# Output projection of the first attention: plain fp32 matmuls in place of split halves

## What is computed

```python
q = einsum('bqm,muh->bquh', h, Wq) + bq     # h = layernorm(x), 32 heads of 64
k = einsum('bkm,mvh->bkvh', h, Wk) + bk     # 8 heads of 64
v = einsum('bkm,mvh->bkvh', h, Wv) + bv
q, k = rope(q) * SCALE, rope(k) * SCALE
scores = where(|i - j| <= 128, q k^T, NEG)  # a sink logit per head is appended
probs = softmax([scores, sink])[..., :-1]
out = einsum('buqk,bkuh->bquh', probs, v)
x = x + einsum('bquh,uhm->bqm', out, Wo) + bo
```

## Time and profile before

| | |
|---|---|
| runs | 1245.62, 1250.10, 1249.98 us (median 1249.98) |
| the profiled execution | 1249.12 us |
| its span, first to last instruction | 1247.3 us |
| mean granted TensorE clock | 0.939 of full speed |
| attention_0 | from 0 to about 378 us of the span |
| steps in its steady part | one each 9.8 to 10.2 us, four in 39.54 us |

### The profile page before, as it was taken

The page is one execution under the profiler, slowest core; times in us unless marked ns, Lnnn a source line. Parts: engine busy times, 40 slices in busy tenths (PEclk is TensorE's granted clock), DMA queues, the critical chain, the costliest instruction groups (busy, mean ns, idle before and its releaser), DMA issues. The chain is left out here.

```text
span 1247.3 us, 21375 instructions
## 1 busy us (share of the span) xinstructions
PE 1052.3 (84%) x7014; PEld 833.8 (67%) x7016; DVE 802.0 (64%) x2260; ACT 646.6 (52%) x1583; POOL 448.6 (36%) x408
## 2 busy tenths in 40 slices
PE   4789999999988986699993799999999977786767
PEld 3556666666665655588882588788887855575556
DVE  5656666666644565355557867677676745489983
ACT  2166676766663751243331566767676642234532
POOL 5456565655634331000002433433343300106730
PEclk8999999999998996799996899999999998898878
DMA  4250212101005000444430001010110000000001
GB/s 135 66 162 18 52 44 51 44 19 35 2 2 193 1 2 0 91 117 111 105 71 13 9 14 34 21 34 17 30 34 21 17 1 0 1 26 26 26 28 45
DMA packets 27246, 53.54 MB, mean 43 GB/s; under 512 B 4565, under 2 KB 11797, under 8 KB 26788
## 3 DMA queue, kind: packets, MB, share of 16 engines
q1 hardware_dynamic: 27172, 52.60, 15.5%
HBM read 42.56 MB, written 1.63 MB: 35 GB/s over the span
## 5 line engine op out<-in xcount | busy, mean ns | idle before, releaser
L382 POOL TENSOR_TENSOR sb_a_P<-sb_a_P,sb_a_rec 128x512 f32<-128x512 f32 x128 | 130.5, 1040 | 134.7 <-DVE sb_a_rec L572 134.7
L459 ACT ACTIVATE sb_a_P<-sb_a_nS,sb_a_nm 128x257 f32<-128x257 f32 x256 | 129.0, 509 | 24.4 <-DVE sb_a_nm L561 24.3
L561 DVE CUSTOM_DVE_ANT_0 sb_a_nS<-a_pS,sb_a_mask,sb_a_nsink 128x256 f32<-128x256 f32 x256 | 107.7, 479 | 15.5 <-PE a_pS L685 15.5
L1723 ACT ACTIVATE sb_a_t<-a_pp,sb_a_w 64x512 f32<-64x512 f32 x128 | 87.5, 684 | 49.4 <-PE a_pp L142 48.1
L468 ACT COPY sb_xn<-a_pT 128x512 f32<-128x512 f32 x128 | 73.7, 576 | 74.7 <-PE a_pT L699 74.5
L142 PE MATMUL a_pp<-sb_x_high,sb_a_w_low 128*128 128x512 f32 x188 | 87.1, 464 | 29.2 <-POOL sb_a_w_low L1661 20.3
L699 PE MATMUL a_pT<-sb_ident,sb_a_P 128*128 128x128 f32 x512 | 82.0, 283 | 18.4 <-ACT sb_xn L468 10.5
L1793 DVE SCALAR_TENSOR_TENSOR sb_a_t<-a_pp,sb_a_w,sb_a_cs 128x512 f32<-128x512 f32 x64 | 47.8, 746 | 73.9 <-ACT sb_a_t L1723 73.9
L699 PEld LDWEIGHTS a_pT<-sb_ident,sb_a_P 128*128 128x128 f32 x512 | 54.4, 142 | 52.1 <-issue 42.0
L142 PE MATMUL a_pY<-sb_a_wo_high,sb_a_OT_low 128*128 128x256 f32 x256 | 79.2, 309 | 7.6 <-DVE sb_a_OT_low L135 5.3
L130 ACT CAST sb_a_OT_high<-a_pO 128x256 fp32r<-128x256 f32 (+1 forms) x96 | 42.6, 444 | 78.1 <-PE a_pO L1936 39.2
(11 more groups left out here) (359 smaller groups left out, 3242.8 us busy)
## 6 DMA issues: line engine op xcount, KB each, us to landing
sb_m_cw<-m_table SPq DMA_DIRECT2D x17, 512.0 KB
sb_a_kr<-sb_a_kall SPq DMA_DIRECT2D x56, 128.0 KB, 2.4
sb_f_w<-f_w SPq DMA_DIRECT2D x12, 384.0 KB, 3.0
sb_m_gu<-m_gu SPq DMA_DIRECT2D x17, 256.0 KB, 6.5
sb_a_w<-a_w SPq DMA_DIRECT2D x16, 257.0 KB, 2.7
sb_m_dn<-m_dn SPq DMA_DIRECT2D x17, 128.0 KB, 6.7
sb_a_w<-a_w SPq DMA_DIRECT2D x8, 259.0 KB, 2.7
sb_a_wo<-a_wo SPq DMA_DIRECT2D x8, 256.0 KB, 2.6
```

The source lines that it names most:

```text
L382: nc.gpsimd.tensor_tensor(part, part, rec[b % 2][:, h, :].rearrange("p (q o) -> p q o", o=1) .to_broadcast([P, 2, S]), ALU.mult).then_inc( ...
L459: out = nc.scalar.activation(Pm[b % 2][:, h, qt, 0:S + 1], nS[:, h, qt, 0:S + 1], ACT.Exp, bias=nm[b % 2][:, h, qt:qt + 1], scale=-1.0, ac ...
L561: out = nc.vector.tensor_tensor_reduce(nS[:, h, qt, 0:S], pS[h][:, qt * S:(qt + 1) * S], wmask[:, qt, :], -1.0, nsink[par][:, h:h + 1], AL ...
L1723: out = nc.scalar.activation(t2[n][a, :, :].rearrange("p b s -> p (b s)"), pp[n][b, :], ACT.Identity, bias=bias[b])
```

## The change

The output projection no longer works on split halves. OT is one fp32 tile for each parity, which ACT copies out of pO; the DVE and POOL subtractions and the ACT rounding of wo are gone; project_out reads wo as it was loaded and issues two plain fp32 matmuls for each half where it issued six fp32r ones. Since wo is now read by the matmuls themselves, the load of wo[g] into its buffer waits for projected instead of wo_split.

```diff
-        both = parts("wo", [P, 2 * KD * D])
-        wos = [[g[:, i * KD * D:(i + 1) * KD * D] for g in both] for i in range(2)]
-        wks = both
+        wks = parts("wk", [P, 2 * KD * D])
...
-        OT = [parts(f"OT{i}", [P, NC]) for i in range(2)]
+        OT = [sb(f"OT{i}", [P, NC]) for i in range(2)]
...
                 sp.dma_start(w[g % 2][:, :], src["a0_w"][g]).then_inc(w_in[g % 2], 16)
-                sp.wait_ge(wo_split, g - 1)
+                sp.wait_ge(projected, (g - 1) * NB)
                 sp.dma_start(wo[g % 2][:, :], src["a0_wo"][g]).then_inc(wo_in[g % 2], 16)
...
-                    if b == 1:
-                        wo_low(G, par)
...
-            def high_OT(G, b):
+            def evac_OT(G, b):
                 act.wait_ge(weighed, G * (2 * NB) + (2 * b + 2))
                 if some(G, b, 2):
                     act.wait_ge(projected, G * NB + (b - 1))
-                high_of(nc, OT[b % 2][0][:, :], pO[:, :]).then_inc(OT_high, 1)
+                nc.scalar.copy(OT[b % 2][:, :], pO[:, :]).then_inc(OT_ready, 1)
...
                     if some(G, b, 2):
-                        high_OT(*lagged(G, b, 2))
-                    if b == 1:
-                        wo_to_high(G, par)
+                        evac_OT(*lagged(G, b, 2))
...
-            def low_OT(G, b):
-                dve.wait_ge(OT_high, G * NB + (b + 1))
-                low_of(nc, OT[b % 2][1][:, :], pO[:, :], OT[b % 2][0][:, :]).then_inc(OT_ready, 1)
...
-            low_OT(A0_G - 1, NB - 2)
             add_y(A0_G - 1, NB - 3)
-            low_OT(A0_G - 1, NB - 1)
             add_y(A0_G - 1, NB - 2)
...
                     if b == 0:
-                        pe.wait_ge(wo_split, G + 1)
+                        pe.wait_ge(wo_in[par], halves(G))
...
                 for p in range(2):
-                    out = split_product(nc, pY[:, qt * D:(qt + 1) * D],
-                                        [g[:, p * S + qt * P:p * S + (qt + 1) * P] for g in OT[b % 2]],
-                                        [g[:, p * D:(p + 1) * D] for g in wos[par]], start=(p == 0), stop=(p == 1))
+                    out = nc.tensor.matmul(pY[:, qt * D:(qt + 1) * D], OT[b % 2][:, p * S + qt * P:p * S + (qt + 1) * P],
+                                           wo[par][:, p * D:(p + 1) * D], start=(p == 0), stop=(p == 1))
```

More of the change, by code:

```diff
@@ L266, in attention_0 @@
                                                    sem("normed"))
-        turnedP, PT_ready, weighed, OT_high, OT_ready = (sem("turnedP"), sem("PT_ready"), sem("weighed"), sem("OT_high"),
-                                                         sem("OT_ready"))
+        turnedP, PT_ready, weighed, OT_ready = sem("turnedP"), sem("PT_ready"), sem("weighed"), sem("OT_ready")
         projected, added, bo_in, rstd_ready = sem("projected"), sem("added"), sem("bo_in"), sem("rstd_ready")
-        w_high, w_split, wo_high, wo_split = sem("w_high"), sem("w_split"), sem("wo_high"), sem("wo_split")
+        w_high, w_split = sem("w_high"), sem("w_split")
         wk_high, wk_split, wv_high, wv_split = sem("wk_high"), sem("wk_split"), sem("wv_high"), sem("wv_split")
@@ L357, in w_low @@
                 low(w_high, G + 1, w[par][:, 0:A0_NQ], [g[:, :] for g in ws[par]], w_split)
-            def wo_low(G, par):
-                low(wo_high, G + 1, wo[par][:, :], wos[par], wo_split)
             def rotate(n, tt, out, done):
@@ L431, in w_to_high @@
                 high_of(nc, ws[par][0][:, :], w[par][:, 0:A0_NQ]).then_inc(w_high, 1)
[L433 to L439, removed]
             act.wait_ge(wk_in, 32)
@@ L491, in _ @@
                 body(G, G % 2, last=(G == A0_G - 1))
-            high_OT(A0_G - 1, NB - 2)
+            evac_OT(A0_G - 1, NB - 2)
             for h in range(A0_R):
                 evac_PT(A0_G - 1, NB - 1, h)
-            high_OT(A0_G - 1, NB - 1)
+            evac_OT(A0_G - 1, NB - 1)
         @block.vector
@@ L588, in body @@
                 for b in range(NB):
-                    if some(G, b, 2):
-                        low_OT(*lagged(G, b, 2))
                     for h in range(A0_R):
```

## The result

The changed kernel takes 1271.16 us (median of 4, 1268.55 to 1273.39) against 1250.04 us for the kernel before (median of 4): a ratio of 1.0177, 95% interval 1.0144 to 1.0209, 21.1 us slower. The profiled execution took 1272.70 us with a span of 1270.9, which is 23.6 us over the one of before.

A forecast was written before the change was run, and what follows sets the result against it. ACT's chain was taken to bound the head of each attention_0 step, PE the tail. 10.0 + 4.6 + 1.5 - 1.1 = +15.0 us on 1249.12 gave 1264 us, range 1257 to 1274.

The forecast's parts named there:

- the end of the stage: Last output projection of attention_0: with the vector work gone, the last add starts earlier, -1.1 us.
- The products: project_out in attention_0: a half of two plain fp32 matmuls takes 0.86 us, hidden under ACT's chain, worth 0.
- Rival (c): Stall plus dearer product bare in project_out, 4 or 17 us: 1268 to 1281; chance 0.08 for over 1274.
- (b): Head of a step paced by PE; plain matmuls save 9 us, plus 1.1 at the end: 1239 without stall; chance 0.07.
- The removed vector work: Subtractions on DVE and POOL and casts on ACT in attention_0 lie in slack, worth 0 in the steps.
- The moved wait, g = 2: SP's later wait before loading wo[2] delays w[3], so ACT's evac_PT in step (1, 3) comes late: +10.0 us.
- The moved wait, g = 3 to 6: SP's later wait delays w[g + 1] in four later groups, +1.15 us each, +4.6 in all, bounds 4 to 8.
- The clock: PE's idling in step (1, 3) drops its clock to 1.2 GHz, +1.5 us, bounds 0 and 3.

The follow-up runs named there:

- extra-matmul run: Changed kernel with SP loading wo last, plus one plain fp32 matmul more in every half of project_out: 1263.34 us, ratio 1.0139.
- fetch-ahead run: Changed kernel with the 13 fetches for later stages issued ahead of SP's wait for projected: 1259.48 us, ratio 1.0093.
- w-before-keys run: Changed kernel with the load of w[g + 1] issued ahead of the eight key copies, behind wo[g] and the fetches: 1255.62 us, ratio 1.0068.
- wait-alone run: Kernel before, products still split, with only SP's wait before loading wo[g] changed from wo_split to projected: 1276.36 us, ratio 1.0211.

## Why the prediction was right, and by how much it fell short

The time, 1271, lies in the range of 1257 to 1274, and the mechanism was the one forecast. The size was not: 21.1 us measured between medians, 23.6 between the profiled executions, where the sum said 15.0. That 1271 still lies in the range is in part luck: the later groups went 1.4 us over their bounds of 4 to 8 us even without the clock, the end of the stage gave back less than the 1 us counted on, and the total kept inside because g = 2 stayed 2 us below its own upper bound.

**The products, worth 0: right.** The half costs 0.86 us, as the run with one more matmul shows where nothing hides it. Passing from transposes to plain matmuls costs the 0.08 us that was the upper bound: 202.14 - 201.65 = 0.49 us against 0.41 in the earlier trace rows. Sum 1.35 under a chain of 1.42. Of the 0.15 us to spare there 0.07 are left, and the extra-matmul run confirms it with 0.06. Rival (c) fell with it, and so did (b): nothing in a quiet step moved by more than 0.02 us. The three passes of the split product, beside (c), are this kernel's own code: split_product with its three fp32r matmuls of 0.12 us.

**The removed vector work, worth 0 in the steps: right.** The end of the stage was put at -1.1. The part reckoned, from the last copy of pO to the last add, is 1.08 us shorter:

```profile
397.89 0.59 ACT L458 COPY sb_a_OT<-a_pO 128x512 f32<-128x512 f32 x1 [2.51 <-PE a_pO L683]
398.53 1.99 PE L695 MATMUL a_pY<-sb_a_wo,sb_a_OT 128*128 128x256 f32 x8 [0.69 <-ACT sb_a_OT L458]
400.56 0.69 DVE L562 TENSOR_TENSOR sb_x<-a_pY,sb_x 128x512 f32<-128x512 f32 x1 [3.00 <-PE a_pY L695]
```

That is 2.67 us, against 3.75 in the earlier trace rows. But the copy itself starts 15.26 us behind the last step's first transposes, where it was 14.82: in the drain, where ACT has no exponentials left, a plain half delays what follows it. Net -0.6; half of the term of -1.1 was lost there.

**The moved wait, g = 2.** Up to the issue the working held: SP noticed projected 2.95 us behind the step's transposes (2.94 said), the fetches took 7.7 us (8.0), the keys 5.25 (5.97), w[3] left 16.4 us behind them (17.3). The term that was mis-sized is the landing: 2.65 us taken from w on an idle queue, 5.9 measured, since the fetches were still being moved (DMA share 0.53 from 127.80 to 141.50, rows below; 3.0 us with the fetches long done). The row that showed it, m_dn's 5.3 us in the earlier trace rows, stood in the bounds and not in the sum. evac_PT came 12.4 us late, not 10.0. The fetch-ahead run takes the fetches away, the w-before-keys run the keys, and each shows its part.

**The moved wait, g = 3 to 6.** 1.15 us each were said, 4.6 in all; the steps grew by 10.6. In step (2, 3) evac_PT came 181.19 - 167.72 = 13.47 us behind the transposes of (2, 2), where 10.47 is due and 11.6 was said. The key copies took 6.54, 6.26, 5.59 and 4.95 us to issue against 5.1, w landed after 2.9, 2.8, 2.8 and 3.5 against 2.65, and w's own issue comes 0.1 us behind the keys. The bounds, 4 to 8 us for the four, didn't reach it. The step that fell short is the same for both: durations of issues and landings were taken from a queue that was quiet and used for one that has just been handed a batch. For g = 3 to 6 the late copies come to 9.4 us of the 10.6, and the clock to 1.2.

**The clock, +1.5: right for step (1, 3), left out for (2, 3).** Busy time by stretch, columns as in the earlier trace rows:

```profile
124.10:127.80 3.70, 1.52 (x12) 1.07 (x8) 3.32 (x16) 0.00 (x0) 0.76 (x1) 1.00 0.88 272
127.80:141.50 13.70, 3.62 (x13) 3.18 (x14) 0.79 (x2) 3.67 (x11) 1.91 (x2) 0.50 0.53 133
...
178.50:182.40 3.90, 1.01 (x8) 0.63 (x7) 2.46 (x14) 1.74 (x5) 1.04 (x1) 1.00 0.33 84
182.40:185.80 3.40, 3.40 (x13) 2.70 (x11) 0.77 (x2) 2.49 (x9) 1.52 (x3) 0.50 0.00 0
...
221.00:235.00 14.00, 11.36 (x95) 7.54 (x87) 6.89 (x25) 7.67 (x23) 6.98 (x7) 1.00 0.15 39
```

After the long stall PE works at 1.2 GHz until 141.5, and the step loses 13.85 - 12.4 = 1.5 us more than the late copy. That this is the 1.5 said is partly luck: the same difference is 1.4 us in the wait-alone run and 2.1 in the w-before-keys run, whose copy comes 7.8 us late. After the 3 us stall of (2, 3) it does so for 3.4 us, and the step loses 4.16 - 3.0 = 1.2. I had reckoned with the clock for the long stall alone. The Trainium skill, "TensorE: Matmul & The Clock Gate", "What's actually happening", has idleness lower the clock; the trace agrees, for the granted clock fell to 0.50 behind both stalls. It didn't fall behind the other three of this kernel (1.00, the last row shows (3, 3)), whose copies came 2.6, 1.9 and 2.0 us late and whose steps lost no more than that. The length of the stall doesn't decide it here: the wait-alone run has copies 2.47 and 2.40 us late in (2, 3) and (4, 3), which lost just that, and 2.37 and 2.55 us late in (3, 3) and (5, 3), which lost 3.44 and 3.68. Its rows of (3, 3), (4, 3) and (5, 3):

```profile
224.00:227.40 3.40, 3.40 (x15) 2.67 (x13) 0.77 (x2) 2.92 (x10) 1.77 (x2) 0.50 0.00 0
...
264.00:268.00 4.00, 1.84 (x15) 1.70 (x16) 1.68 (x10) 3.22 (x10) 1.28 (x1) 1.00 0.07 26
309.40:312.80 3.40, 3.27 (x14) 2.46 (x13) 0.77 (x2) 2.62 (x10) 2.04 (x2) 0.50 0.00 0
```

So the price is 1.1 to 1.3 us a time in the runs with short stalls, and whether it comes due no run here explains. The fetch-ahead run paid it behind a copy 2.3 us late (129.90 to 133.30 at 0.50). The step it was taken from in the earlier trace rows is as unsteady: (0, 2) takes 11.0 us in three of the eleven traces, in two it is (0, 1), and in six neither.

**The sum as it came out**, from the profiled executions: 12.4 + 1.5 for (1, 3), 10.6 for the four others with 1.2 of clock in it, -0.6 at the end, and -0.3 from the start: 23.6 us.

## What to carry to other kernels

When an operand is no longer copied before use, its buffer is free later, and so is the wait of whoever refills it: list everything that the refilling queue issues behind that wait, and compare each item's landing with the moment at which its first user comes for it. On a queue that issues in order, put the waits that end last behind everything that is due sooner, or give the operand one buffer more so that they end sooner; the same instructions in another order were worth 22 to 27 us here, against about 2 us, not clear of noise, for all the arithmetic that was removed. Price transfers behind a batch with the rows of a batch, not with those of an idle queue.

## What the runs showed of the hardware

A plain fp32 matmul of 128x128 weights and 256 columns costs 0.43 us back to back at full clock (two from 156.78 to 157.65 in the run with one more matmul), against 3 x 0.12 = 0.36 for the three fp32r matmuls that replace it, so splitting saves only 0.07 us of PE for each product. Passing from transposes to plain fp32 matmuls took 0.08 us more than passing to fp32r ones (0.49 against 0.41), and passing back took nothing: in the run with one more matmul the transposes start 0.87 us after the last pair began, four records of 0.215.

The eight key copies took SP 4.95 to 6.67 us to issue in these runs, one after the other, while a load of w took 0.33 us alone. w, of 259 KB, landed 2.6 to 2.8 us after its issue on a quiet queue, 2.8 to 4.1 right behind the eight copies, and 5.9 to 7.0 behind the 13 fetches.
